# Attention with a value product behind every unit, or two of them back to back behind every second one

## The reference

```python
qkv = jnp.einsum('bsm,qhdm->qbhsd', x, W_qkv)
scores = jnp.einsum('bhqd,bhkd->bhqk', Q, K)
scores = jnp.where(causal_mask, NEG_INF, scores) * scale
attn = jax.nn.softmax(scores, axis=-1)
ctx = jnp.einsum('bhqk,bhkd->bhqd', attn, V)
```

## Time and profile before

| | |
|---|---|
| median of three runs | 2794.82 us |
| lowest, highest run | 2787.42, 2795.98 us |
| profiled execution | span 2796.0 us |
| head groups between the first and the last `max_turn` | 287.7 to 2039.6 us |
| last group | 2039.6 to 2139.4 us |
| PE, DVE, ACT busy over the span | 90%, 78%, 62% |

### The profile page before, as it was taken

One profiled execution on the slowest core, in us unless ns is written; L12 is line 12 of the kernel. 1 busy time (PEld: TensorE's weight loads), 2 busy tenths in 40 slices (PEclk: granted clock), 3 DMA queues, 4 the chain that ended last, 5 costly groups with the idle time before them and its releaser, 6 DMA issues. The chain is left out here.

```text
span 2796.0 us, 49392 instructions
## 1 busy us (share of the span) xinstructions
PE 2529.9 (90%) x16192; PEld 1298.9 (46%) x16192; DVE 2179.1 (78%) x5287; ACT 1727.6 (62%) x3481; POOL 692.7 (25%) x721
## 2 busy tenths in 40 slices
PE   7978999999999999999999999999996579999990
PEld 6852333333333333333333333333332479999990
DVE  6979889888888788888888898888821867777761
ACT  4640576777666666666666667666674257777760
POOL 3453333000010101011010110101012435556553
PEclk9986899999999999999999999999998689999995
DMA  6989788412404234040431404234012635555548
GB/s 213 316 280 301 275 282 286 145 27 57 97 28 97 56 73 116 13 117 29 96 92 37 120 22 104 52 78 105 16 54 84 217 84 92 88 90 91 91 68 255
DMA packets 218336, 331.82 MB, mean 119 GB/s; under 512 B 27408, under 2 KB 158224, under 8 KB 218096
## 3 DMA queue, kind: packets, MB, share of 16 engines
q1 hardware_dynamic: 137728, 170.48, 21.4%
q0 software_dynamic: 58704, 136.86, 19.7%
q10 hardware_dynamic: 21664, 21.50, 2.5%
HBM read 140.75 MB, written 187.20 MB: 117 GB/s over the span
## 5 line engine op out<-in xcount | busy, mean ns | idle before, releaser
L1007 ACT ACTIVATE probs<-ps 128x512 f32<-128x512 f32 (+3 forms) x2400 | 1122.2, 539 | 587.5 <-PE ps L1335 339.4
L1033 DVE TENSOR_REDUCE early<-ps 128x1 f32<-128x512 f32 x1536 | 1001.5, 684 | 106.0 <-PE ps L1240 100.1
L1240 PE MATMUL ps<-kh,qs 96*128 96x512 bf16 (+3 forms) x2560 | 882.2, 361 | 88.0 <-DVE early L1033 37.4
L1335 PE MATMUL ps<-qs,kh 99*128 99x512 bf16 (+3 forms) x2560 | 831.1, 352 | 17.0 <-ACT probs L1007 6.6
L1351 PE MATMUL ps<-probs,vs 128*32 128x512 f32 (+3 forms) x5120 | 605.8, 545 | 0.0
L1240 PEld LDWEIGHTS ps<-kh,qs 96*128 96x128 bf16 x2560 | 250.7, 99 | 700.5 <-DVE early L1033 303.6
L1029 DVE CUSTOM_DVE_ANT_0 junk<-ps,causal 128x128 bf16<-128x128 f32 (+3 forms) x1024 | 480.7, 483 | 52.8 <-PE ps L1240 48.0
L1335 PEld LDWEIGHTS ps<-qs,kh 99*128 99x128 bf16 x2560 | 246.1, 98 | 290.7 <-ACT probs L1007 135.8
L1760 POOL DMA_INDIRECT acc<-y,to x156 | 250.6, 1606 | 119.0 <-ACT y L1815 73.9
L926 POOL DMA_INDIRECT rows_out<-row,place_a x96 | 95.2, 991 | 698.5 <-DVE place_a L697 650.8
L1339 PE MATMUL ps<-ident_b,causal_b 128*128 128x128 bf16 x1024 | 214.0, 221 | 0.0
(11 more groups left out here) (231 smaller groups left out, 3011.2 us busy)
## 6 DMA issues: line engine op xcount, KB each, us to landing
rows_out<-row POOLq DMA_DIRECT2D x129, 544.0 KB, 3.6
xg<-rows_out SPq DMA_DIRECT2D x39, 544.0 KB
v_ones<-vt SPq DMA_DIRECT2D x16, 1024.0 KB, 6.4
vs<-v_ones SPq DMA_DIRECT2D x16, 1024.0 KB, 11.2
contexts<-ctx_out SPq DMA_DIRECT2D x64, 256.0 KB
q_parts<-parts SPq DMA_DIRECT2D x32, 384.0 KB, 4.6
k_parts<-parts SPq DMA_DIRECT2D x32, 384.0 KB, 4.6
qs<-q_parts SPq DMA_DIRECT2D x64, 192.0 KB, 7.3
```

Of the source, the lines that this page charges most:

```text
L1007: nc.scalar.activation(probs[u % PB][:, h, q0:TB], bank(s % SB)[:, q0:TB], ACT.Exp, scale=SCALE).then_inc(exp_done, 1)
L1033: nc.vector.tensor_reduce(early[:, h, t, k0 // CW:k0 // CW + 1], tile, AX.X, ALU.max).then_inc(max_done, 1)
L1240: nc.tensor.matmul(tile[:, 0:w], qh[a % HR][0:STACK, t * P:(t + 1) * P], kh[a % HR][0:STACK, k0:k0 + w], start=True, stop=True).then_inc(m ...
L1335: mm = nc.tensor.matmul(tile[:, q0:TB], kh[a % HR][:, kt * P:(kt + 1) * P], qh[a % HR][:, j * TB + q0:(j + 1) * TB], start=True, stop=not ...
```

## The change

In `step`, the call of `p_v` in the middle of every unit goes. Behind the four scores of every even unit, and ahead of the unit's last point of chunks, stand two calls, for the two units before. At unit 0 these are the last two units of the group before. After the last group two calls follow as before. The order of scores and chunks among themselves is the same, and all waits inside `p_v` are the same. No other engine's order changes.

```diff
@@ -1366,14 +1366,16 @@
                         chunks(POINTS * u)
                         score(g, u, 1)
                         chunks(POINTS * u + 1)
-                        if u >= LAG:
-                            p_v(g, u - LAG)
-                        elif g:
-                            p_v(g - 1, NU - LAG + u)
                         chunks(POINTS * u + 2)
                         score(g, u, 2)
                         chunks(POINTS * u + 3)
                         score(g, u, 3)
+                        if u % 2 == 0:
+                            for behind in range(LAG, 0, -1):
+                                if u >= behind:
+                                    p_v(g, u - behind)
+                                elif g:
+                                    p_v(g - 1, NU + u - behind)
                         chunks(POINTS * u + 4)
                         if u == TURN and g + 1 < NG:
                             max_turn(g + 1)
```

## The result

The changed kernel takes **2950.61 us** (median of 4 runs, 2941.13 to 2960.32), beside 2792.28 for the kernel before. The ratio is 1.0572, 95% interval 1.0545 to 1.06: 158 us slower, three times the forecast and outside its range.

A forecast was written before the change was run, and what follows sets the result against it. PE was taken to bound plain groups, with DVE and ACT close behind. Plain groups +6, worked groups +27, turn +6 and last group +10 made +49 on 2796: 2845 us; range 2790 to 2880, leaving out the faster rival.

The forecast's parts named there:

- part one: On PE, pairing 40 p_v into 20 pairs saves 0.24 us each, 4.8 us a group, if PE alone counts.
- part two: PE's longer silence at each pair leaves DVE dry for 0.5 us; a plain group grows by 1.4 us, four by 6.
- windows: The 20 stretches from pair to pair in a group, each bounded by PE's work, PSUM banks emptied by DVE, or ACT.
- plain group: A head group without work for a finished batch in its stream; 103.7 us before, PE busy all but 0.2 us.
- the ring: Four PSUM banks shared by chunks and emptied in order by DVE; cover 2.27 us, against 2.80 us around a pair.
- four of them: The four groups before the worked ones, all counted as plain groups at +1.4 us each, together +6 us.
- Worked groups: Head groups with a finished batch's work on DVE; ten of 119.9 us each before, PE idle 5.8 us in each.
- part three: In worked groups DVE already bounds eight windows, so pairs cost +2.4 us a group (1.4 to 3.4), +27 over 11.
- part four: After `max_turn`, cover for line 812's DMAs is 1.1 us shorter; six groups with six DMAs lose 1.0 each, +6 us.
- part five: In the last group, with scores in two banks of two, some 13 full pairs cost 0.8 us each, +10 us.
- The faster rival: PE alone counts, the ring does not bind and only seams are saved: 2734 us, 2770 with half; chance 0.19.
- What would show it: Signs listed beforehand: DVE idle 0.4 to 0.6 us at every pair, plain groups 105 us, worked 122, last 110.

The follow-up runs named there:

- three banks: Chunks in three PSUM banks in place of four, one run in each kernel: 3070.85 us in the changed kernel, 2916.99 us in the kernel before.

## Why the prediction was wrong

**The direction, and the reason given for it, were right; the sum was a third of the change.** By its own steps:

- **Seams (part one).** Right: a pair takes 1.86 us to the next chunk, where one p_v takes 0.99, and a second one would have added 0.1 of entry and 0.99. And as forecast, almost none of it reached the end.
- **Silence and ring (part two).** Right in mechanism, as three banks showed, and small by 3 us a group: +1.4 forecast, +4.5 measured. Window by window (from score to score, a unit earlier than the forecast's windows) part of the plain group came out near the working: units 16 and 17 grew by 0.67 us (forecast 0.68), 26 and 27 by 0.49 (0.47), 28 and 29 by 0.24 (0.19). But 14 and 15 grew by 0.55 (0.21), 32 and 33 by 0.68 (0.09), 34 and 35 by 0.60 (0.3), and 2 and 3 by 0.20, 20 and 21 by 0.32 and 36 and 37 by 0.41, where a gain was forecast; 30 and 31 grew by 0.23 only (0.65), and 12 and 13 and 24 and 25 gained where a small loss was forecast. The step that failed is the assumption that a window is bound by the last chunk's bank alone, or by PE. Scores wait for ACT within it as well (0.9 us in the group, 0.2 before), and narrow chunks empty the ring; which of the two made up the rest was not taken apart. I called these "four of them" as well for the groups before the plain one; those have DVE work of their own (gates), their clock went from 0.98 to 0.96, and they lost 23 us, not 4.
- **Worked groups (part three).** This is the step that was wrong: "+2.4 a group ... Bounds 1.4 and 3.4". Measured 11.6 in each of ten and 9.4 in the one before them, 126 us in place of +27. About half of it is the clock, 5 to 7 us a group, a term that the sum does not have at all; what pairs cost with the clock up lies between 2.9 and 7.2, so that the ring's part was probably too small as well. The forecast did not see how near PE is to its lower clock: it read "the clock is at its upper level throughout" as a fact of the kernel, while the runs show it for a p_v in every unit (1.00 in the middle, 1.00 at the end with ACT's copy moved) and not for pairs. It asked what fills DVE's wait, and never what fills PE's. The kernel before could have told: the first worked group, which stands between the plain group and the ten in the earlier trace rows and was left out of them, is 4.5 us longer than those with the clock at 1.00, and its own is 0.96.

```profile
716.69:840.57 123.88, 118.27 (x757) 43.99 (x756) 103.51 (x275) 80.79 (x171) 13.26 (x17) 0.96 0.28 71
```

- **The turn (part four).** Forecast +6: the waits for line 812's DMAs ahead of a group's first score rose from 0.9 to 4.8 us (the kernel's very first group aside), in five of the six groups with six DMAs. Right in kind, and +3.9 in size. One of them, against the earlier trace rows:

```profile
1018.83 0.39 PE L1335 MATMUL ps<-qs,kh 99*128 99x512 bf16 x1 [1.66 <-DMA qs<-neg]
```

- **The last group (part five).** Forecast +10, measured +9.6, and +10.7 in the run that changed it alone.
- **The faster rival** needed PE alone to count. In the windows that part two left to PE it should have held in any case, and the run with pairs only there was 0.7% slower.
- **What would show it:** of the marks, plain groups of 105, worked of 122 and last of 110 were given; they came out at 108, 131 and 109. DVE's dry spells were given as 0.4 to 0.6 us and are often near 1.1. "PE busy less" went the other way: 2589.4 us in place of 2529.9, and 104.8 in place of 103.5 in the plain group.

What stays open: how the clock decides, and so why it came down at a wait of 1.68 us and at one of 1.59 that had mostly left it up before. The runs say that it was lowest where pairs at the units' ends met DVE's batch work (0.94), higher with one of the two changed (0.98 with pairs in the middle and with no pairs where DVE has that work, 1.00 with singles at the end), and that extra matmuls brought it back in the changed kernel (1.00, with a fall in two of ten groups) but lowered it a little in the kernel before (0.99).

## What to carry to other kernels

Work on PE that stands between waits can be what keeps its clock up; before moving it, look at which waits it fills on PE itself, and not only at the engines that wait for PE. Where two engines are both close to the bound, time saved on one in a window where it is the bound can be lost again in the next, as here 0.23 us saved and 0.36 lost. A clock that reads 1.00 as the mean of ten groups can hide falls in single ones: read it group by group. And an experiment that moves one operation has to move whatever on other engines was placed by its old position.

## What was not expected of the hardware

PE's clock fell from 2.4 to 1.2 GHz within a stage where PE is busy 90% of the time, near 1470.5, within a wait of 1.68 us and behind 3.6 us in which PE had been busy for 2.27. It fell at 1494.4 behind 3.5 us in which PE never waited, the last of them the router's small matmuls, and in the kernel before it stayed up around a wait of 1.59 us with PE busy for 2.09 of 3.6. The two levels showed in one line's rows: a pair of products 1.92 and 3.64 us, a matmul of 512 columns 0.38 and 0.61 to 0.63. 36 matmuls, whose results nobody reads, made a worked group 4.5 us shorter.

The Trainium skill, in TensorE: Matmul & The Clock Gate, under HAM oscillation, ties the lower clock to gaps in which PE idles between bursts of matmuls. The trace agrees in kind for the fall at 1470.5, but that group's longest wait of PE, 1.68 us, is shorter than the gaps of which the section speaks; the fall at 1494.4 had no such gap ahead of it.
